# Scores of element 0 straight from T, with the bias rows added by a whole fp32 matmul over four rows

## The reference

```python
B, S, C_IN, M = (8, 256, 32, 16)          # C_OUT = 32, N_HEADS = 8, C_H = 256
Q = Wq x + bq; K = Wk x + bk; V = Wv x + bv   # 32 -> 256 channels, x = _gn(x)
QK = Qp @ Kt                  # for each b, m: (256 x S) @ (S x 256)
A = jax.nn.softmax(QK, axis=-1)
out = jnp.einsum('bmcC,bmsC->bsCm', A, Vp)
return x + (Wo out + bo)      # einsum sums A over its first channel index
```

## Time and profile before

| | us |
|---|---|
| median of 3 runs | 199.22 |
| lowest, highest | 196.81, 209.14 |
| the profiled execution | 199.71 |
| its span, first to last instruction | 197.9 |

### The profile page before, as it was taken

How to read it: one execution, slowest core, us unless ns; L and a number is a source line. 1 busy time by engine, 2 the same in 40 slices (tenths; PEclk the granted TensorE clock), 3 DMA queues, 4 the chain that set the end, 5 groups by cost and what they waited for, 6 DMA issues and landing times. The chain is left out here.

```text
span 197.9 us, 5954 instructions
## 1 busy us (share of the span) xinstructions
PE 165.7 (84%) x2208; PEld 89.7 (45%) x2208; DVE 130.8 (66%) x291; ACT 128.8 (65%) x529; POOL 99.5 (50%) x122
## 2 busy tenths in 40 slices
PE   0697096999897899999999999989897898799753
PEld 0263035555454545564545455535454453464330
DVE  0355429748886788778777878788778766654241
ACT  0200005957798688788868887988798998874401
POOL 3353656404897299497558755963642303214000
PEclk9999758569999999999999999999999999955975
DMA  5900585893299169639933972588079502200202
GB/s 192 365 6 0 108 196 96 199 239 146 31 199 252 66 131 205 210 62 197 260 137 58 208 206 81 76 196 264 12 128 215 201 0 109 103 6 0 106 5 106
DMA packets 9626, 26.61 MB, mean 134 GB/s; under 512 B 2459, under 2 KB 3326, under 8 KB 9598
## 3 DMA queue, kind: packets, MB, share of 16 engines
q1 hardware_dynamic: 8224, 25.57, 50.1%
q10 hardware_dynamic: 1374, 0.67, 1.3%
HBM read 9.06 MB, written 4.19 MB: 67 GB/s over the span
## 5 line engine op out<-in xcount | busy, mean ns | idle before, releaser
L772 ACT ACTIVATE e_sb<-s_bank,negmax 128x256 f32<-128x256 f32 x256 | 117.6, 495 | 49.6 <-DVE negmax L584 27.9
L584 DVE TENSOR_REDUCE negmax<-s_bank 128x2 f32<-128x512 f32 x128 | 87.1, 686 | 24.4 <-PE s_bank L404 23.1
L404 PE MATMUL s_bank<-stack,wq_st 99*128 99x256 f32 x256 | 63.2, 341 | 3.7 <-ACT e_sb L772 2.5
L404 PEld LDWEIGHTS s_bank<-stack,wq_st 99*128 99x128 f32 x256 | 39.8, 201 | 41.0 <-issue 40.7
L772 ACT ACTIVATION_READ_ACCUMULATOR e_sb<-s_bank,negmax 128x1 f32 x256 | 58.1, 227 | 0.0
L414 PE MATMUL acc<-e_sb,recip 128*32 128x256 f32 x512 | 43.4, 412 | 9.4 <-DVE recip L590 8.9
L815 POOL TENSOR_TENSOR xc<-xs,nm 128x512 f32<-128x512 f32 x15 | 15.9, 1082 | 20.1 <-DVE nm L543 20.1
L866 POOL TENSOR_TENSOR t_parts<-t_sb,t_parts 128x1280 fp32r<-128x1280 f32 x7 | 20.4, 2908 | 4.3 <-DVE t_parts L579 3.8
L565 DVE SCALAR_TENSOR_TENSOR t_sb<-bk_sb,ssum,bz 128x256 f32<-128x256 f32 x28 | 12.9, 465 | 12.4 <-PE bz L382 10.4
L879 POOL TENSOR_TENSOR ws<-wo_sb,aT 128x1024 f32<-128x1024 f32 x7 | 13.4, 1912 | 14.2 <-DVE aT L600 14.2
L414 PEld LDWEIGHTS acc<-e_sb,recip 128*32 128x32 f32 x512 | 10.7, 111 | 20.8 <-DVE recip L590 13.8
(11 more groups left out here) (72 smaller groups left out, 128.8 us busy)
## 6 DMA issues: line engine op xcount, KB each, us to landing
stack<-t_parts SPq DMA_DIRECT2D x32, 256.0 KB, 4.9
xs<-x_rows SPq DMA_DIRECT2D x8, 512.0 KB, 5.7
stack<-t_parts SPq DMA_DIRECT2D x32, 128.0 KB, 4.8
xT<-x_cols SPq DMA_DIRECT2D x8, 512.0 KB, 6.0
y_cols<-yb SPq DMA_DIRECT2D x7, 512.0 KB, 4.1
y_cols<-yb SPq DMA_DIRECT2D x2, 256.0 KB, 2.0
stack<-t_parts SPq DMA_DIRECT2D x8, 32.0 KB
k_sb<-consts ACTq DMA_DIRECT2D x1, 235.5 KB, 4.5
```

The source lines that it names most:

```text
L404: mm = nc.tensor.matmul(s_bank[p % NS][:, CH * h:CH * h + CH], wq_st[:, P * h:P * h + P], stack[:, side, p % Q, p // Q, :], start=True, st ...
L584: nc.vector.tensor_reduce(negmax[:, p % NS, :], s_bank[p % NS][:, :].rearrange("p (h n) -> p h n", h=HC), op=ALU.max, axis=AX.X, negate=Tr ...
L772: last = nc.scalar.activation(e_sb[:, p % NE, h, :], s_bank[p % NS][:, CH * h:CH * h + CH], ACT.Exp, bias=negmax[:, p % NS, h:h + 1], accu ...
```

## The change

Element 0's scores no longer use the stack. `score_first` multiplies the 32 rows of T for the position by a full-precision copy of Wq (`wq_sb`, repeated for each q), as a whole fp32 matmul on the 32-row group q, and adds the bias rows by a second whole fp32 matmul into the same accumulation: four rows of the partitions of q, `tb_rows` (from a `tb_product_first` of 128 columns) against `bq_rows` (bq masked by t, made by GpSimd). Two halves are issued together: half 1 of position p and half 0 of position p + 1, which stand on different row groups and in different banks; first both products, then both bias products. The second half of each position thus comes a slot's worth later than its first, and the scores at a slot wait for one exponential more than before.

With it: `stack_up(0)`, `high_part(0)`, `low_part_first` and their twelve-row bias go; element 1's T products, its reads, its high part and `split_wq` (the split of the stacked Wq) move from the opening into slots 0 to 9; element 2's chain, which began in the opening, moves to slots 2 to 19; element 3's anchor goes from slot 22 to 24, element 4's from 36 to 37. Element 1's statistics use the bank `acc` and not `s_bank[2]`, `gnorm` and `ssum` get a second side, `read_t` signals after each of its four reads, half of `centre_rows(1)` goes to VectorE (`centre_chunk(1)`), `wobv` is made later, and three loads change (`bq_rep` and `wq_rep`, 128 KB each, are new). Its core:

```diff
-ANCHOR = {2: 7, 3: 22, 4: 36, **{j: M * (j - 2) + 3 for j in range(5, B)}}
...
+ANCHOR = {0: 0, 1: 1, 2: 13, 3: 24, 4: 37, **{j: M * (j - 2) + 3 for j in range(5, B)}}
...
+NEVER = -1000
+HI_FIRST, SPLIT_WQ = 6, 9
 EARLY = {
-    2: {**CHAIN, **dict(gram=-7, variance=-4, read_gram=-6, sum_diagonal=-5, read_variance=-3)},
-    3: {**CHAIN, **dict(sum_rows=-17, mean=-14, gram=-10, sum_groups=-16, read_mean=-13)},
-    4: {**CHAIN, **dict(sum_rows=-18, mean=-15, sum_groups=-17, read_mean=-14)},
+    0: {**dict.fromkeys(CHAIN, NEVER), **dict(t23_product=0, read_t2=0, read_t3=1)},
+    1: {**dict.fromkeys(CHAIN, NEVER), **dict(t01_product=0, tb_product=1, t23_product=3,
+                                              read_t0=1, read_t1=2, read_tb=2, read_t2=3, read_t3=4)},
+    2: {**CHAIN, **dict(sum_rows=-11, mean=-9, gram=-6, variance=-4, sum_groups=-11, read_mean=-9,
+                        read_gram=-5, sum_diagonal=-4, read_variance=-3)},
+    3: {**CHAIN, **dict(sum_rows=-13, mean=-11, gram=-9, variance=-5, sum_groups=-12, read_mean=-10,
+                        read_gram=-7, sum_diagonal=-6, read_variance=-4)},
+    4: {**CHAIN, **dict(sum_rows=-16, mean=-13, gram=-10, sum_groups=-15, read_mean=-12, read_gram=-8, sum_diagonal=-7)},
+    5: {**CHAIN, **dict(sum_rows=-18, sum_groups=-17)},
 }
...
@@ -279,23 +297,13 @@
                     src = t_parts[0:2 * M, side, 0, T, :] if part == 0 else t_parts[0:M, side, 1, T, :]
                     sp.dma_start(dst.bitcast(f32), src.bitcast(f32)).then_inc(bias_stacked[side], 16)
-                if j == 0:
-                    high(0)
-                    bias(0)
-                    sp.wait_ge(parts_done, 1)
-                    low(0)
-                    bias(1)
-                    for q in range(1, Q):
-                        high(q)
-                        low(q)
-                else:
-                    for q in range(Q):
-                        high(q)
-                    bias(0)
-                    sp.wait_ge(parts_done, j + 1)
-                    bias(1)
-                    for q in range(Q):
-                        low(q)
+                for q in range(Q):
+                    high(q)
+                bias(0)
+                sp.wait_ge(parts_done, j)
+                bias(1)
+                for q in range(Q):
+                    low(q)
             def store(j):
                 sp.wait_ge(y01_read, j + 1)
...
@@ -304,9 +312,8 @@
             for j in range(4):
                 load_rows(j)
-            stack_up(0)
+            load_cols(0)
             stack_up(1)
-            load_cols(0)
             for b in range(B):
                 if b >= 3:
                     store(b - 3)
...
@@ -390,15 +399,38 @@
                 nc.tensor.matmul(by[0:2 * M, 0:CH], sblk[:, :, :, :].rearrange("p k q t -> p (k q t)"), wk_sb[:, :],
                                  start=True, stop=True).then_inc(tb_mm, 1)
+            def tb_product_first():
+                pe.wait_ge(sblk_done, 1)
+                nc.tensor.matmul(by[:, 0:CH], sblk_first[:, :, :, :].rearrange("p q k t -> p (q k t)"), wk_sb[:, :],
+                                 start=True, stop=True).then_inc(tb_mm, 1)
+            def score_first(halves):
+                for p, h in halves:
+                    t, q = p // Q, p % Q
+                    pe.wait_ge(t_read, t + 1)
+                    after(pe, exped, p - NS + 1)
+                    rows = slice(C * q, C * q + C)
+                    nc.tensor.matmul(s_bank[p % NS][:, CH * h:CH * h + CH], wq_sb[rows, P * h:P * h + P],
+                                     t_sb[rows, 0, t, :], start=True, stop=False)
+                for p, h in halves:
+                    t, q = p // Q, p % Q
+                    rows = slice(C * q, C * q + T)
+                    mm = nc.tensor.matmul(s_bank[p % NS][:, CH * h:CH * h + CH], bq_rows[rows, t, P * h:P * h + P],
+                                          tb_rows[rows, :], start=False, stop=True)
+                    if h == HC - 1:
+                        mm.then_inc(scores, 1)
             def score(b, p):
+                if b == 0:
+                    score_first([(p, 1), (p + 1, 0)] if p + 1 < M else [(p, 1)])
+                    return
                 side = b % 2
-                pe.wait_ge(stacked[side][p % Q], 32 * (b // 2 + 1))
-                pe.wait_ge(bias_stacked[side], 32 * (b // 2 + 1))
+                pe.wait_ge(stacked[side][p % Q], 32 * ((b + 1) // 2))
+                pe.wait_ge(bias_stacked[side], 32 * ((b + 1) // 2))
+                if b == 1 and p == 0:
+                    pe.wait_ge(set_dve, 2)
                 n = M * b + p
-                if n == 1:
-                    pe.wait_ge(t23_done, 2)
-                if n == 2:
-                    pe.wait_ge(vare_done, 2)
                 after(pe, exped, n - NS + 1)
                 for h in range(HC):
...
@@ -410,6 +442,8 @@
                     pe.wait_ge(inverted, T * b + t + 1)
                     if t == 0:
                         after(pe, acc_read, b)
+                    if b == 0 and t == 0:
+                        pe.wait_ge(vare_done, 2)
                 for q in range(Q):
                     mm = nc.tensor.matmul(acc[C * q:C * q + C, 0:CH], recip[:, t, q, h, :],
...
@@ -505,20 +541,17 @@
             gram_of(0)
             mean(1)
             variance(0)
-            sum_rows(2)
-            pe.wait_ge(w_loaded, 16 * 7)
+            pe.wait_ge(w_loaded, 16 * 8)
             t_product(0, 0, t01_mm, bz)
-            tb_product(0)
-            t_product(0, 2, t23_mm, t23_bank(0))
+            tb_product_first()
             gram_of(1)
-            mean(2)
+            pe.wait_ge(bq_done, 1)
+            pe.wait_ge(tb_done, 1)
+            score_first([(0, 0)])
+            score(0, 0)
+            score(0, 1)
             variance(1)
-            t_product(1, 0, t01_mm, bz)
-            tb_product(1)
-            t_product(1, 2, t23_mm, t23_bank(1))
-            pe.wait_ge(set_dve, 2)
-            for p in range(AHEAD):
-                score(0, p)
+            score(0, 2)
             for b in range(B):
                 element(b)
             for h in range(HC):
...
                 dve.wait_ge(t01_mm if t < 2 else t23_mm, j + 1)
                 dve.wait_ge(ssum_done, j + 1)
-                after(dve, parts_done, j - 1)
+                after(dve, parts_done, j - 2)
+                if j == 2:
+                    dve.wait_ge(scores, M)
                 src = bz if t < 2 else t23_bank(j)
-                mm = nc.vector.scalar_tensor_tensor(t_sb[:, j % 2, t, :], bk_sb[:, :], ssum[:, t:t + 1],
+                mm = nc.vector.scalar_tensor_tensor(t_sb[:, j % 2, t, :], bk_sb[:, :], ssum[:, j % 2, t:t + 1],
                                                     src[:, CH * (t % 2):CH * (t % 2) + CH], ALU.mult, ALU.add)
-                if t % 2 == 1:
-                    mm.then_inc(t01_done if t < 2 else t23_done, 1)
+                mm.then_inc(t_read, 1)
             def read_tb(j):
                 dve.wait_ge(tb_mm, j + 1)
-                after(dve, parts_done, j - 1)
+                after(dve, parts_done, j - 2)
                 nc.vector.scalar_tensor_tensor(t_sb[0:2 * M, j % 2, T, :], bk_sb[0:2 * M, :], rows_all[0:2 * M, :],
...
@@ -636,6 +670,10 @@
                     if slot >= Q + 1 and p % Q == 1:
                         n = (slot - Q - 1) // Q
                         invert(n // T, n % T)
+                    if slot == HI_FIRST:
+                        high_part(1)
+                    if slot == SPLIT_WQ:
+                        split_wq()
                     if b >= 3 and p == 0:
                         read_y23(b - 3)
                     if (j := due("sum_groups", slot)) is not None:
...
@@ -670,15 +708,16 @@
                     if last and p == at["read_y23_second"]:
                         read_y23(b - 1)
-            def centre_first():
-                dve.wait_ge(mean_done, 1)
+            def centre_chunk(j):
+                dve.wait_ge(mean_done, j + 1)
+                after(dve, gram_mm, j)
                 shift = nm[:, :, None, None].to_broadcast([P, G, M // G, C])
                 nc.vector.tensor_tensor(xc[:, 0, :, 0:C].rearrange("p (g k) c -> p g k c", g=G),
-                                        xs[:, 0, 0].rearrange("p (g k) c -> p g k c", g=G), shift, ALU.add
...
+            centre_chunk(0)
             sum_groups(1)
             diagonal_first()
             read_gram(0)
@@ -714,28 +753,17 @@
             read_mean(1)
             read_variance(0)
             scaled_first()
-            sum_groups(2)
-            split_wq()
-            dve.wait_ge(set_pool, 1)
+            centre_chunk(1)
+            dve.wait_ge(w_loaded, 16 * 8)
+            dve.wait_ge(set_zeros, 2)
             read_t(0, 0)
+            read_tb_first()
+            read_gram(1)
             read_t(0, 1)
-            read_tb(0)
-            read_t(0, 2)
-            read_t(0, 3)
```

(33 more changed lines are left out.)

87 lines of the change are left out of this document (54 added, 33 removed).

## The result

The changed kernel takes 227.9 us, the median of four executions (226.4 to 230.3); the kernel before, on the same chips, 200.3. The ratio is 1.148, with a 95% interval of 1.129 to 1.168: slower by 15%, where I had forecast 198.0 us and no change that can be told, with a range up to 204.5. Ratios here are of the fast executions alone, since some executions of the same kernel take some per cent longer at a lower granted clock.

What follows compares the result with a forecast made beforehand. TensorE's pace was taken as the bound. The terms put element 2's first score at 65.8 + 0.7 = 66.5 us against 67.7, 1.2 earlier: 199.7 - 1.2 = 198.5, with the profile 0.5 above the median 198.0 us, range 194 to 204.5.

Steps and rivals of the forecast that it cites:

- The bound and the mark: The loop runs at TensorE's pace; the change is worth how much earlier than 67.7 us element 2's first score comes.
- more is kept: Rival, 0.22: stacks come sooner (3.6 us at slot 29) or the end's half-clock stretch vanishes (4.1 less); about 194.5 us.
- The clock in the opening: Before slot 0: a late rise to full clock costs 0.7 us, with ends 0 and 1.4.
- a clock that stays full through element 0: A sign, in element 0, that would show the forecast's steps to be right.
- Slots 0 to 12: Element 0's slots before the first score from element 1's stack: 21.0 us, 12.6 for pairs and 8.4 for other work.
- Pairs side by side: Element 0's score pairs: two halves on different row groups run together, 0.99 us a pair with the change of shape.
- unpaired halves: Rival, 0.13: in element 0 pairs run one after the other, 1.86 us in place of 0.99; 206.5 us.
- loads or order not hidden: Rival, 0.08: weight loads or in-order starts add one or two steps of 0.216 us a pair; 198 to 201 us.
- Element 1's stack: Before slot 13: the stack lands at 44.4 us, so TensorE waits 2.6 us for it.
- Slots 13 to 28: From element 1's first stack score to element 2's first score: 4.6 us for slots 13 to 15, 16.7 for 16 to 28.
- the chains stall: Rival, 0.12: SP queue, row loads or VectorE's maxima delay either stack by 2 to 4 us; 200.5 to 202.5 us.
- about 11 us of the first exponential's 12.5 are given back in element 0: Element 0: of the first exponential's 12.5 us gain about 11 are lost, as 19.4 us there becomes some 27.

Runs made afterwards that it cites:

- e3_open: The changed kernel with extra whole fp32 matmuls, results overwritten, filling TensorE's idle time of the opening; 221.2 us.
- e1_bias32: The changed kernel with element 0's bias matmuls taking all 32 rows of their row group instead of four, the other 28 zero; 215.1 us.
- e9_one_whole: e3_open with each pair's two four-row bias matmuls replaced by one over all 128 rows, for half 1 alone; 206.1 us.
- e10_power_first: e9_one_whole with GpSimd making element 3's power, scaled_gram and scaled_sums ahead of element 2's low part, in element 0; 202.7 us.
- e2_nobias: The changed kernel without element 0's 32 bias matmuls; 215.7 us.
- e12_before_fill_timed: The kernel before with extra matmuls in the opening's idle time and one in each of slots 0 to 9 of element 0; 193.9 to 208.1 us.
- e5_rows128: The changed kernel with element 0's products and bias products over all 128 rows instead of 32 and four; 215.7 us.
- e6_fill: The changed kernel with e3_open's fills, e1_bias32's 32-row bias matmuls and one extra matmul in each slot of element 0 but slot 3; 209.0 us.

## Why the prediction was wrong

**The bound and the mark** were right in the main: the loss arose before slot 29. Behind it the loop took 127.6 us against 130.2, which I had as equal. The last element's stretch at half clock lasted 3.4 us (202.9 to 206.3) in place of 10.3, so the second half of the rival "more is kept" came true in part; that fits the 2.6 us, where I had priced it at 4.1. The loss ahead of slot 29 drowned it.

**The clock in the opening** was a term of the sum, 0.7 us, with 0 and 1.4 as its ends. That is the step that failed, and with it the two terms worked out at full clock, 21.0 for slots 0 to 12 and 21.3 for slots 13 to 28: the clock stayed at half to 80.0 us, and they took 41.2 and 33.2. I let the clock rise either at 16 us or some us later, and worked out all slots "at full clock". The third possibility, that it doesn't rise at all while TensorE is wholly busy, was nowhere among the rivals; "a clock that stays full through element 0" was only a sign to look for. The end of 1.4 us was too small as well: slot 0 is at 20.1 with the clock up in e3_open and at 23.9 without. My reason, that the opening idles 1 us where before it was busy, isn't shown: e1_bias32 idles there as much (1.11 us) and its clock rose at 17.7. But a clock that is up at 14.7 falls at 21.6 all the same.

Why I missed it: I read "TensorE busy" as "clock up". The earlier trace rows had the warning in it, 9.61 of 10.20 us busy at half clock from 33.0 us, and 10.30 of 10.30 from 172.9. I used both as prices and didn't ask what they meant for 13 slots of narrow matmuls. The Trainium skill, page "TensorE: Matmul & The Clock Gate", Part 1, describes the gate by how busy TensorE has recently been; in this case's traces that is not enough, with 40.00 of 40.00 us busy at half clock.

**Slots 0 to 12**: 21.0 forecast, 41.2 measured (23.9 to 65.1), the ratio of the two clocks but for a few per cent. By kinds at half clock: a pair 2.00 us (28.45 to 30.45) against 0.99, a T product 1.86 against 0.99, a column sum about 1.0 against 0.57. In e9_one_whole, at full clock, the slots take 26.1: 21.0, 3.4 for pairs of 1.26 in place of 0.99, and 1.7 for the wait of `variance(2)` on element 2's trace. So the list of work was right, and each price was right at the clock for which it was read.

**Pairs side by side**: right. 1.06 against 0.99. The rival of unpaired halves (1.86) and the one of loads or order not hidden (1.2 to 1.4 a pair) are out. The Trainium skill, page "TensorE: Matmul & The Clock Gate", Part 3, lets a load overlap a running matmul only where the row group differs and has matmuls start strictly in order; the eight records of 0.216 in 1.06 us are four rounds side by side and do not agree with that. (The same part also names a background weight buffer that a load may go to ahead of time, which would agree; no run here shows it.)

**Element 1's stack**, to be waited for 2.6 us: no wait at all in the kernel after, since the slots between its high part and slot 13 took twice as long. In e9_one_whole TensorE doesn't wait for it either: slot 13, at 46.8, is late enough by itself.

**Slots 13 to 28**: 21.3 forecast. 33.2 in the kernel after, at half clock but for 8.1 us; 27.0 in e9_one_whole, of which 4.5 are waits listed there and about 1.8 the half clock from 55.0 to 58.5. Here the rival "the chains stall" was right in kind: its place is GpSimd's queue, not the SP queue or the stack.

**A slip in the prediction.** That about 11 us of the first exponential's 12.5 are given back in element 0 doesn't fit its own numbers: 19.4 us becoming some 27 gives back under 8 there, and the rest goes behind it. The sum doesn't use it.

**What the change is worth without the clock.** e9_one_whole is at 206.1 us; less 2.5 for its dearer pairs and 1.8 for its half-clock stretch that would be 202, some 3 us over the kernel before, worked out and not run. The larger part of what separates it from my forecast is the waits, which my sum had only in part. But e10_power_first, alike up to slot 29, was at 202.7, so a single execution doesn't settle 3 us. And both have the opening filled, with which the kernel before takes 194.4. So nothing here speaks for a gain at full clock, and whether the change alone would then be slower can't be told; the 26 us between 202 and the 227.9 measured are the clock's.

What stays open: how tall or wide the matmuls must be, and for what share of the time, so that the clock holds. The runs order the cases (four rows, 32 rows in two groups, one of them over 128 rows) and give no rule. Tall matmuls don't settle it either: once down, the clock stayed at half for 15 us of stack scores in the kernel after (14.40 us busy), in e1_bias32 and in e2_nobias, and for 20.5 us in e12_before_fill_timed. Several falls come in or just behind a wait of TensorE of about 2 us (the kernel after at 86.8, e1_bias32 at 41.6, e5_rows128 at 74.8, e10_power_first at 68.6), but the one of e3_open at 21.6 doesn't. Bias matmuls of 128 rows, all but four of them zero, which would compute the right scores, were not run, so the values in the added rows may matter too. Single executions stand behind most rows of the table, and the clock's own falls differ from one execution to the next.

## What to carry to other kernels

Narrow matmuls can cost twice: in a stretch where most of TensorE's time goes into matmuls of four to 32 rows, check its clock before pricing anything, and price the stretch at both clocks. Read the clock from the duration of an instruction that occurs at both levels and not from the clock line alone, above all ahead of the first record. And where a matmul of few rows may as well be one of 128 at the same number of steps, the tall one is worth a try: it held the clock here, at 0.2 us a pair for the change of shape.

## What the runs showed of the hardware

- The granted clock does not follow how busy TensorE is. Busy 40.00 of 40.00 us and at half clock: pairs of 32-row and four-row matmuls. Busy 38.41 of 38.90 us and at full clock: the same over 128 rows. Fallen from full to half while never idle: e3_open at 21.6 us. Busy 20.50 of 20.50 us and at half clock with the loop's scores of 99 rows: e12_before_fill_timed.
- Exchanging two four-row matmuls side by side for one of 128 rows, at the same number of steps, was worth 12.8 us at slot 13 (one execution each, on two chips).
- When the clock rises in the opening differs between executions of the same instructions: at 17.7 us in e1_bias32, and not at all in the kernel after and e2_nobias, which are alike up to there.
- Extra work can be a gain: 16 extra matmuls in idle time made the kernel before 1.8% faster; 15 more, with bias matmuls of 32 rows, made e6_fill 12 us faster than e3_open (one execution each).
- Two whole fp32 matmuls of 128 columns of weights on neighbouring row groups run wholly side by side: 1.06 us for eight records of 0.216.
